# Linear attention in a Perceiver block: float32 query features in 32-row tiles, and attention computed transposed

## The reference

```python
qkv = x @ w_qkv                                  # x after layer norm, D = 512
q, k, v = heads of 32 values, 16 heads
elu1(x) = where(x > 0, x + 1, exp(x))
q_proj = elu1(einsum('bhnd,hdf->bhnf', q, proj))  # 128 features a head
k_proj = elu1(einsum('bhnd,hdf->bhnf', k, proj))
kv     = einsum('bhnf,bhnd->bhfd', k_proj, v)
attn   = einsum('bhnf,bhfd->bhnd', q_proj, kv)
z      = 1 / (einsum('bhnf,bhf->bhn', q_proj, sum of k_proj over n) + 1e-8)
out    = (attn * z) as rows of 512, @ w_out + b_out
```

## Time and profile before

| what | value |
|---|---|
| time, median of three runs | 705.38 us |
| the profiled execution: its own time, its span | 705.94 us, 704.1 us |
| PE busy | 668.0 us, 95% of the span |
| DVE busy, ACT busy | 296.6 us (42%), 233.9 us (33%) |
| chain that ended last: PE, DVE, ACT, DMA | 79%, 10%, 4%, 3% |
| linear attention, from the first query projection to the output product | 317.2 to 381.3 us |
| mean granted TensorE clock | 0.987 of 2.4 GHz |

### The profile page before, as it was taken

One profiled execution on the slowest core, in us unless ns is written; L12 is line 12 of the kernel. 1 busy time (PEld: TensorE's weight loads), 2 busy tenths in 40 slices (PEclk: granted clock), 3 DMA queues, 4 the chain that ended last, 5 costly groups with the idle time before them and its releaser, 6 DMA issues.

```text
span 704.1 us, 10065 instructions
## 1 busy us (share of the span) xinstructions
PE 668.0 (95%) x4112; PEld 401.6 (57%) x4112; DVE 296.6 (42%) x611; ACT 233.9 (33%) x444; POOL 33.6 (5%) x35
## 2 busy tenths in 40 slices
PE   6989999999999999799988899999999999999977
PEld 5767778787777875578966554333333333333322
DVE  5965544626445265666875653212121211202111
ACT  4644545545354452456771121011101011010110
POOL 0300000000000000570000100000000000000000
PEclk9999999999999999899999899999999999999998
DMA  8111011010700000303086703589999999999961
GB/s 310 64 61 61 21 41 61 1 61 1 299 1 2 1 1 2 105 1 131 1 354 272 330 0 120 181 330 410 373 397 380 390 393 392 366 402 364 408 219 61
DMA packets 14347, 129.68 MB, mean 184 GB/s; under 512 B 2720, under 2 KB 2848, under 8 KB 6240
## 3 DMA queue, kind: packets, MB, share of 16 engines
q1 hardware_dynamic: 12384, 127.09, 46.8%
q10 hardware_dynamic: 1920, 1.97, 1.0%
HBM read 126.03 MB, written 1.05 MB: 180 GB/s over the span
## 4 chain that ended last, share of the span: by engine, by line
PE 79%; DVE 10%; ACT 4%; DMA 3%; issue 1%; ACTq 1%; SPq 1%; DVEq 0%
PE ps L977 21%; PE ps L1235 14%; PE ps L1242 7%; PE ps L1271 7%; PE ps L1156 4%; PE ps L1280 4%; PE ps L1047 4%; PE ps L1023 2%; PE ps L1058 2%; DMA eo_slot<-eo 2%; PE ps L1088 2%; PE ps L1193 2%; PE ps L1205 1%; ACTq L595 1%; DVE stats L644 1%
## 5 line engine op out<-in xcount | busy, mean ns | idle before, releaser
L872 DVE TENSOR_TENSOR hid<-hid,ps 128x512 f32<-128x512 f32 x24 | 16.5, 687 | 140.5 <-PE ps L1235 94.0
L1271 PE MATMUL ps<-w_d,hid_T 128*64 128x512 f32 x256 | 58.1, 595 | 1.4 <-ACT hid_T L601 1.4
L586 ACT ACTIVATE hid<-ps 128x512 f32<-128x512 f32 x24 | 14.3, 597 | 134.8 <-PE ps L1235 98.2
L1235 PE MATMUL ps<-w_u,x_slot 128*64 128x512 f32 x256 | 58.1, 596 | 1.0 <-DVE give_last L948 1.0
L1235 PE MATMUL ps<-w_g,x_slot 128*64 128x512 f32 x256 | 58.1, 595 | 0.0
L474 ACT ACTIVATE probs<-ps,neg_max 128x512 f32<-128x512 f32 x64 | 43.5, 688 | 39.1 <-DVE neg_max L724 39.1
L977 PE MATMUL ps<-wv_hi,ctx_hi 128*128 128x512 f32 x128 | 51.7, 404 | 0.1
L704 DVE COPY probs_T<-ps 128x512 f32<-128x512 f32 x32 | 22.1, 692 | 68.7 <-PE ps L1047 68.7
L977 PE MATMUL ps<-wv_lo,ctx_hi 128*128 128x512 f32 x128 | 50.0, 391 | 0.0
L977 PE MATMUL ps<-wv_hi,ctx_lo 128*128 128x512 f32 x128 | 49.9, 390 | 0.0
L724 DVE TENSOR_REDUCE neg_max<-ps 128x1 f32<-128x512 f32 x64 | 39.7, 682 | 18.4 <-PE ps L1023 18.3
(11 more groups left out here) (192 smaller groups left out, 1117.8 us busy)
## 6 DMA issues: line engine op xcount, KB each, us to landing
w_u<-in_wu SPq DMA_DIRECT2D x16, 2048.0 KB, 15.1
w_d<-in_wd SPq DMA_DIRECT2D x16, 2048.0 KB, 10.2
w_g<-in_wg SPq DMA_DIRECT2D x16, 2048.0 KB, 12.1
ctx_raw<-in_ctx SPq DMA_DIRECT2D x7, 1024.0 KB, 4.9
w_qkv<-in_wqkv SPq DMA_DIRECT2D x1, 3072.0 KB, 15.2
ws_g<-in_wsg SPq DMA_DIRECT2D x1, 2048.0 KB, 7.7
ws_u<-in_wsu SPq DMA_DIRECT2D x1, 2048.0 KB, 7.7
ws_d<-in_wsd SPq DMA_DIRECT2D x1, 2048.0 KB, 22.2
```

The costliest lines, as they stand in the source:

```text
L1235: ins = pe.matmul(ps[64 * fh:64 * (fh + 1), dst, :], x_slot[:, dt, e, :], weights[e % 2][:, dt, BANK * fh:BANK * (fh + 1)], start=(dt == 0 ...
L1271: ins = pe.matmul(ps[64 * fh:64 * (fh + 1), 6 + n % 2, :], hid_T[:, n % 2, j, 64 * fh:64 * (fh + 1)], w_d[e % 2][:, KT * fh + j, :], start ...
```

## The change

Six parts. The query projection is kept in float32 (`q_l`, one copy by ScalarE) instead of being split. Query features are computed from it in float32: the four heads of a channel tile lie in four groups of 32 rows, each head's 128 features are two halves of 64, and the eight matmuls (32 rows, 64 columns stationary, 512 tokens moving) are issued together as four units. Feature units from the ninth on rotate over six banks (2, 0, 1, 5, 6, 7). `KVW` is 34. Attention is computed with 32 value columns of `kv` stationary and 64 tokens of query features moving, and the sums by a second set with the column of sums repeated 32 times as stationary, so that the result already has channels as rows: the 16 transposes and four copies go. VectorE takes the reciprocal of the repeated sums, 128x256, and multiplies. All eight attention steps stand at the end of the list. `ws_d` is loaded after `w_g0`, both behind the last attention step. `act_relus` is true for every second unit throughout.

The diff, without the layout of buffers, renumbered constants and semaphores:

```diff
-KVW = 48
+KVW = 34
-        LN_BANK, RES_BANK = (2, 4, 0), (0, 4)
-        ATT_BANK = (0, 1, 2, 7)
+        LN_BANK, RES_BANK = (2, 4, 0), ((0, 1, 2, 3), (5, 6, 7, 4))
...
-        LIN_ORDER = [("p", 8, 0), ("k", 0, 0), ("k", 0, 1), ("p", 9, 0), ("k", 0, 2), ("k", 0, 3), ("p", 10, 0), ("p", 11, 0)]
...
-        def act_relus(u):
-            return u % 2 == 0 or u >= NT * KT
-        for t in range(NT):
-            LIN_ORDER += [("q", 2 + t // 2, 2 * t % 4), ("q", 2 + t // 2, 2 * t % 4 + 1), ("att", 0, t)]
-        LIN_ORDER += [("att", 1, t) for t in range(NT)]
-        QKV_BY = [("dve",)] * 4 + [("act", "dve")] * 4 + [("dve",)] * 4
+        LIN_ORDER = [("p", 8, 0)] + four("k", 0) + [("p", 9, 0)] + four("k", 1) + [("p", 10, 0), ("p", 11, 0)]
+        LIN_ORDER += four("kv", 0)[:2] + four("q", 0) + four("kv", 0)[2:]
+        LIN_ORDER += woven(four("k", 2), four("kv", 1)) + four("q", 1)
+        LIN_ORDER += woven(four("k", 3), four("kv", 2)) + four("q", 2) + four("kv", 3) + four("q", 3)
+        LIN_ORDER += [("att", i, half) for i in range(KT) for half in range(2)]
+        FEAT_BANK = [u % 3 if u < 8 else (2, 0, 1, 5, 6, 7)[(u - 8) % 6] for u in range(len(UNIT))]
+        def act_relus(u):
+            return u % 2 == 0
+        QKV_BY = [("dve",)] * 4 + [("act", "dve")] * 4 + [("act",)] * 4
...
@@ SyncE @@
+            sp.wait_ge(att_done, 2 * KT)
+            sp.dma_start(w_g0[:], wg_d[0]).then_inc(wg_in[0], 16)
             sp.dma_start(ws_d[:], wsd_d).then_inc(wsd_in, 16)
-            sp.wait_ge(att_done, 2 * NT)
-            sp.dma_start(w_g0[:], wg_d[0]).then_inc(wg_in[0], 16)
...
@@ ScalarE @@
                     act.wait_ge(feat_ps, u + 1)
+                    if u >= 3:
+                        act.wait_ge(feat_done, u - 2)
...
                 elif kind == "p":
-                    heads_high(i, ql_halves, i - 8)
-            for dt in (0, 2):
-                act.wait_ge(attT_ps, dt + 1)
-                act.copy(att_T[:, dt, :], bank(ATT_BANK[dt])).then_inc(attT_act, 1)
+                    act.wait_ge(qkv_ps, i + 1)
+                    act.copy(q_l[:, i - 8, :], bank(qkv_bank(i))).then_inc(qkv_act, 1)
+                else:
+                    act.wait_ge(att_ps, a + 1)
+                    act.activation(den[:, a % 2, :], ps[:, 3 + a % 2, TOK // 2:TOK], ACT.Identity, bias=den_eps[:, 0:1],
+                                   scale=1.0).then_inc(den_done, 1)
+                    a += 1
...
@@ VectorE @@
-                elif kind == "p":
-                    heads_low(i, ql_halves, i - 8)
...
-                    dve.wait_ge(att_ps, a + 1)
...
-                    link(dve.reciprocal(den_inv[:, a, :], den[:, a, :]))
...
+                elif kind == "att":
+                    rows = slice(TOK // 2 * r, TOK // 2 * (r + 1))
+                    dve.wait_ge(den_done, a + 1)
+                    link(dve.reciprocal(den[:, a % 2, :], den[:, a % 2, :]))
+                    dve.tensor_tensor(att_T[:, i, rows], ps[:, 3 + a % 2, 0:TOK // 2], den[:, a % 2, :],
+                                      ALU.mult).then_inc(att_done, 1)
                     a += 1
-            for dt in (1, 3):
-                dve.wait_ge(attT_ps, dt + 1)
-                dve.tensor_copy(att_T[:, dt, :], bank(ATT_BANK[dt])).then_inc(attT_dve, 1)
...
@@ TensorE @@
+                    if k == 1 and t % 2 == 0:
+                        pe.wait_ge(att_done, 2 * KT - 1 + t // 2)
...
+                elif kind == "q":
+                    if r == 0:
+                        qkv_out(8 + i)
+                        for j in range(HPT):
+                            feature_bank_free(u + j)
+                        for j in range(HPT):
+                            dims = slice(HD * j, HD * (j + 1))
+                            for side in range(2):
+                                feats = slice(64 * side, 64 * (side + 1))
+                                ins = pe.matmul(ps[feats, FEAT_BANK[u + j], :], proj_twice[dims, 2 * i + j // 2, feats],
+                                                q_l[dims, i, :], start=True, stop=True)
+                            ins.then_inc(feat_ps, 1)
+                    u += 1
...
-                    for h in range(2 * HPT):
-                        ins = pe.matmul(ps[:, 3 + 2 * (a % 2) + h // HPT, 2 * KVW * (h % HPT):2 * KVW * (h % HPT + 1)],
-                                        q_feat[:, 8 * i + h, P * r:P * (r + 1)], kv[:, r, 8 * i + h, :],
-                                        start=True, stop=True)
+                    for b in range(B // 2 * r, B // 2 * (r + 1)):
+                        t, side, col = b // 2, b % 2, L * (b % (B // 2))
+                        for off, cols in ((0, None), (TOK // 2, HD)):
+                            for j in range(HPT):
+                                h = HPT * i + j
+                                if cols is None:
+                                    weights = kv[:, t, h, KVW * side:KVW * side + HD]
+                                else:
+                                    weights = kv[:, t, h, KVW * side + HD:KVW * side + HD + 1].to_broadcast([P, HD])
+                                ins = pe.matmul(ps[HD * j:HD * (j + 1), 3 + a % 2, off + col:off + col + L], weights,
+                                                q_feat[:, h, L * b:L * (b + 1)], start=True, stop=True,
+                                                skip_group_check=True)
...
-                for dt in range(KT):
-                    ins = pe.transpose(ps[:, ATT_BANK[dt], P * t:P * (t + 1)], att[:, t, P * dt:P * (dt + 1)], ident[:])
```

More of the change, by code:

```diff
@@ L111, in perceiver_block @@
         k_feat0 = sb(linear, "k_feat0", [P, NT, HPT * FEAT])
+        k_feat1 = sb(linear, "k_feat1", [P, NT, HPT * FEAT])
+        k_feat = (k_feat0, k_feat1)
+        v_bd = sb(linear, "v_bd", [P, NT, H, 2, KVW])
+        proj_twice = sb(linear, "proj_twice", [P, PAIRS, FEAT])
+        den = sb(linear, "den", [P, 2, TOK // 2])
+        sb(linear, "gap_linear", [P, 256])
+        q_l = sb(linear, "q_l", [P, KT, TOK])
         first = ExitStack()
@@ L1160, in _, with feature_bank_free @@
                 qkv_project(n)
+            def feature_bank_free(u):
+                before = unit_of_bank_before(u)
+                if before is None:
+                    qkv_out(4 + FEAT_BANK[u])
+                else:
+                    pe.wait_ge(feat_done, before + 1)
             u = w = a = 0
@@ L1165, in _ @@
                     qkv_project(i)
[L1166 removed]
+                elif kind == "k":
                     if u == 0:
                         pe.wait_ge(proj_split, 2)
[L1169 to L1180 removed]
+                    feature_bank_free(u)
+                    for pr in range(2):
```

102 lines of the change are left out of this document (32 added, 70 removed).

## The result

The changed kernel took 721.74 us (median of 4 runs, 718.28 to 724.99), the kernel before 705.5 us beside it: a ratio of 1.0231, interval 1.017 to 1.0293. A second measurement gave 720.35 us and 1.0214 (1.0184 to 1.0243). The forecast was 711.5 us. The profiled execution took 724.99 us with a span of 723.2 us. (A ratio leaves out a kernel's runs of over 1.5% above its fastest, a median holds them all; that is why the two part for e9, e16, e17 and e19.)

The account below looks back on a forecast made before the run. TensorE, busy 95% of the span, bounded the kernel, but VectorE's chain would set the changed attention tail. 705.9 plus 3.1 (tail) plus 2.7 (clock) is 711.7, less part of the profiled run's offset: 711.5 us, range 704.5 to 716.5.

Parts of the forecast that it names:

- The clock: In the attention tail, TensorE's 5 us standstill halves its clock: +2.7 us, bounds 0 and 4.4.
- the walk: Stepping three engines' programs through linear attention with estimated durations and waits: last query feature at 369.4 us, good to some 0.7.
- PE's own work: TensorE in linear attention: a query group 1.04 us, an attention step 0.95 us, 10.6 us of work saved besides transposes.
- rival 3: The eight query tiles do not run side by side: 3.5 us a group, 721 us; 0.07 together with Rival 4, large price.
- Rival 4: In attention, the repeated-sum stationary loads slowly: 713 us, or 721 at 3.7 us a step; 0.07 together with rival 3, large price.
- Feature-value steps "priced the same": In linear attention, fewer streamed columns gain nothing because eight weight loads of 0.9 us pace the step.
- Front: First key units and projections: TensorE waits 2.4 us, then 1.1 us; last projection ends at 335.9 us instead of 330.8.
- Middle: From first query feature at 340.1 us to last at 369.4: VectorE waits 6.6 us; TensorE waits 1.8 and 0.8 for kv.
- The reciprocal: Each 128x256 reciprocal on VectorE in the attention steps takes 1.7 us, bounds 0.42 and 2.1.
- Tail: After the last query feature, seven VectorE steps of 2.14 us take 15.0 us; output product starts at 384.3, +3.1 us.
- Transfers: Weight loads released later, at 363.5 us instead of 353.5, still arrive in time: cost 0, at most 10 us.
- Rivals 1 and 2: Reciprocal fast as a plain operation: 702.7 to 708.8 us, chance 0.13; clock stays at 2.4 GHz: 709.1 us, chance 0.14.

Follow-up runs that it names:

- e9: Changed kernel with attention steps reordered (all head tiles of the first 256 tokens first) and half the output product put between the last ones: 715.21 us.
- e16: Changed kernel with the three 2 MB weight transfers started only after the last attention step: 718.19 us.
- e17: e15 with the feature-value steps streaming 68 columns again: 702.41 us, ratio 0.9944 to the kernel before.
- e19: Changed kernel with only the middle reordered: both woven runs first, then query groups two to four with the last four feature-value steps between: 717.79 us.
- e1_wide: Changed kernel with each matmul of a feature-value step streaming 96 value columns where it streamed 68: 713.55 us.
- e10: Changed kernel with 96-column streams, key units and projections alternating in the front, and the reordered tail of e9: 709.07 us.
- e3: Changed kernel with each of the eight reciprocals taken over 8 columns instead of 256, most of the attention left undivided: 710.72 us.
- e14: e12 with the three 2 MB weight transfers started only after the last attention step: 703.34 us.
- e12: Changed kernel with 96-column streams, key units and projections alternating in the front, and reciprocals moved to ScalarE as squared reciprocal square roots: 707.76 us.
- e13: e12 with the middle reordered, both woven runs before query groups two to four: 704.72 us.
- e15: Changed kernel with all helpful edits: 96-column streams, new front, reordered middle, reciprocals on ScalarE, three weight transfers after the attention: 700.77 us, ratio 0.9933.

## Why the prediction was wrong, step by step

- **The clock (+2.7 us, only in the tail): the step that failed.** It looked for a low clock only in the tail, where TensorE stands still for 5 us (4.0 in the trace), and priced the front and the middle at full clock without a word on it. In the tail it came, but so it did at 324.3 and for 34.1 us from 344.8. In the profiled run the front came 2.0 us late (kv steps at 337.89, the walk 335.9), the middle 10.1 us later again (last feature 381.53, the walk 369.4), the tail 3.3 more (18.2 us for 14.9). That is 15.4 us for 2.7, of which the profiled run, 3.3 us above the median, has its share. Where the clock stays up, the rest stands: e1_wide begins the kv steps at 335.76, ends its last feature at 370.2 for a forecast 369.4 and takes 713.55 us for a forecast 711.5, and three of e19's runs of narrow streams take 710.9 to 712.9. That the clock made the miss is shown; what brings it down is shown in part. The term itself was also set by eye: the middle of its bounds 0 and 4.4 is 2.2, not 2.7.
- **PE's own work: right at full clock.** A query group 1.04 us, as forecast. The tiles do run side by side: rival 3 is out. The attention step came at 1.93 us at half clock, against some 1.85 in the forecast; where the clock is up, e16's rows above have 1.10 us as their length, and in e10 the next instruction starts 383.14-382.11 = 1.03 us after a step does, for a forecast of 0.95. Rival 4 is out.
- **Feature-value steps "priced the same": right for the time, silent on what else hangs on it.** Two steps take 340.76 to 342.57 us, 0.90 each, in the changed kernel and 338.65 to 340.46, again 0.90, in e1 with 96 columns. But the long low stretches came only with the narrow stream.
- **Front: right.** Waits of 2.50 and 1.03 us for 2.4 and 1.1.
- **Middle: right by mechanism, but hidden in the profiled run.** There TensorE waits for nothing between 345 us and its first attention steps; at half clock it is itself the limit. The two waits before the last feature-value steps, 1.8 and 0.8 us in the forecast, show where the clock is up there: 1.52 and 0.53 us in e1, 1.54 and 0.55 in e3, whose middle is the changed kernel's own:

```profile
363.59 1.08 PE L1194 MATMUL ps<-v_bd,k_feat 128*128 128x68 f32 x8 [1.54 <-ACT kv L570]
...
365.22 1.08 PE L1194 MATMUL ps<-v_bd,k_feat 128*128 128x68 f32 x8 [0.55 <-DVE kv L838]
```

- **The reciprocal (1.7 us): right.** Its line, with min, median and max in ns, and what VectorE waited for before it (us, times). By (1745-202)/248, from the 128x8 of the earlier trace rows, an element costs 6.2 ns. The estimate from the Trainium skill's "VectorE: DVE Perf Modes", section "First, the fixed hardware budget", was 2.1 to 2.3 us for eight passes; the measurement is 17% below its low end and decides.

```profile
L844 DVE RECIPROCAL den<-den x8: 1743/1745/1753, 381.5 to 399.5; 128x256 f32<-128x256 f32 x8
...
  ACT den L578: 3.0, 3
```

- **Tail: mechanism right, 15.0 us was 18.2.** The rest is the 3.0 us above, in which VectorE waited for ScalarE's copy, behind TensorE at half clock and behind its stop of 1.01 us. In e16, whose last steps have neither, they follow each other at 2.12 us, for 2.14 forecast, and the tail is 15.6. The clock term held 1.5 for this; the stop was in no step. The other 2.9 us of that term, an output product that starts at half clock, did not come: the granted clock is back at 1.0 from 399.4 us on, 0.4 us before the product starts.
- **Transfers (0): right for their arrival**, as e14 shows with 17 us more. But they had a price of another kind, which the forecast put at nothing: late fetches, and with them TensorE's stops. It was a stop of 1.0 us in the changed kernel and 4.4 us once TensorE set the tail.
- **Rivals 1 and 2** needed a fast reciprocal and a clock that stays at 2.4 GHz: neither came.

## What to carry to other kernels

A thinner TensorE program, with less streamed behind each weight load and waits of a microsecond or two between, can run at half its clock over a stretch many times longer, and the busy share then reads 100%: look at the granted clock beside every busy share, and price a thinner TensorE program at both clocks. A repeated value whose reciprocal is taken over all its copies costs VectorE by the copies: 1.75 us for 256 columns; ScalarE had the room. And large transfers that start beside a long run of small matmuls can stop TensorE without a wait that the profile names; start them after it if they are still in time, and look at the instruction queue beside such a stop.

## What the runs showed of the hardware that I had not expected

- With the same instructions the clock falls in one run and not in the next: e19 took 710.9 to 712.9 us in three runs and 722.7 to 725.5 in three, with nothing between. Once down in the middle it stayed down for 34.1 us in four of the traces (changed, e9, e16, e17), with TensorE's records end to end; I can't say what lets it up again.
- A matmul that streams 96 columns behind a weight load takes no longer than one that streams 68 (a step of eight records 0.90 us for both), and may be the cheaper one for the clock: no long low stretch came with it.
- TensorE stops inside the 512 records of the attention, at the same three records in every kernel, for up to 3.7 us, and goes on 1.1 to 1.6 us after a fetch of instructions has landed. With the 2 MB transfers moved away all "issue" stops together fell from 3.1 us (e12) to none in the rows of e14, and from 4.3 (e13) to 1.7 (e15).
